# Cross-attention on one core: value stores issued from ScalarE's queue, loads alone on the sync queue, one bias dot moved in each value tile

## What is computed

```python
qp = q @ Wq + bq                      # q = x, [16, 512, 512]
kp = k @ Wk + bk                      # k = v = ctx, [16, 77, 512]
vp = v @ Wv + bv
w = softmax(einsum('bqd,bkd->bqk', qp, kp) / sqrt(512))
x = einsum('bqk,bkd->bqd', w, vp)
gate = concatenate((qp, x), -1) @ Wg + bg
return x * mask * sigmoid(gate) + q
```

## Time and profile before

| | |
|---|---|
| median of 3 runs | 413.2 us (412.16 to 413.94) |
| the profiled execution, device time | 413.69 us |
| its span in the profile | 411.9 us |
| TensorE matmuls busy | 395.4 us, 96% of the span |
| VectorE busy | 273.2 us, 66% |
| ScalarE busy | 229.6 us, 56% |
| GpSimd busy | 133.3 us, 32% |
| DMA, mean over the span | 223 GB/s |
| matmuls on the chain that ended last | 82% of the span |
| DMA on that chain | 5%, of which `sb_row<-sb_dram` 4% |

### The profile page before, as it was taken

One profiled execution on the slowest core, in us unless ns is written; L12 is line 12 of the kernel. 1 busy time (PEld: TensorE's weight loads), 2 busy tenths in 40 slices (PEclk: granted clock), 3 DMA queues, 4 the chain that ended last, 5 costly groups with the idle time before them and its releaser, 6 DMA issues.

```text
span 411.9 us, 7362 instructions
## 1 busy us (share of the span) xinstructions
PE 395.4 (96%) x2386; PEld 361.6 (88%) x2386; DVE 273.2 (66%) x646; ACT 229.6 (56%) x587; POOL 133.3 (32%) x115
## 2 busy tenths in 40 slices
PE   8999999999993999999999999999999999999993
PEld 4889986777783999999999999999999999999992
DVE  3687558774424667667677676676777766767766
ACT  5644242223313666766666667666666676666643
POOL 0004125434823633243242432423334233333100
PEclk9999999999997999999999999999999999999998
DMA  7993533457496779878788786888978879777321
GB/s 269 390 405 142 148 122 121 155 194 265 142 326 249 227 239 278 236 246 231 229 248 229 251 244 219 236 235 243 250 215 248 241 240 232 233 237 237 113 77 76
DMA packets 42660, 91.79 MB, mean 223 GB/s; under 512 B 4633, under 2 KB 4633, under 8 KB 41983
## 3 DMA queue, kind: packets, MB, share of 16 engines
q1 hardware_dynamic: 41471, 89.23, 69.5%
q10 hardware_dynamic: 1152, 2.10, 1.5%
HBM read 64.30 MB, written 27.01 MB: 222 GB/s over the span
## 4 chain that ended last, share of the span: by engine, by line
PE 82%; DVE 5%; DMA 5%; issue 3%; ACT 3%; POOL 1%; SPq 0%; DVEq 0%; ACTq 0%
PE psum L421 50%; PE psum L341 13%; DMA sb_row<-sb_dram 4%; PE psum L448 4%; PE psum L454 4%; PE psum L447 3%; PE psum L453 3%; PE psum L364 3%; DVE dot_tmp L641 3%; PE psum L433 2%; DMA wkT_raw<-in_wkT 1%; ACT vT L490 1%; POOL v_st L818 1%; POOL xT L818 1%; DVE vg_f L726 1%
## 5 line engine op out<-in xcount | busy, mean ns | idle before, releaser
L421 PE MATMUL psum<-ws,xT 128*128 128x296 f32 x1536 | 229.7, 304 | 0.0
L421 PEld LDWEIGHTS psum<-ws,xT 128*128 128x128 f32 x1536 | 220.8, 190 | 5.6
L818 POOL TENSOR_TENSOR xT<-x_raw,xT 128x512 fp32r<-128x512 f32 x64 | 82.4, 1290 | 150.0 <-ACT xT L608 150.0
L765 DVE SCALAR_TENSOR_TENSOR gx<-psum,rinv,gx 128x512 f32<-128x512 f32 x64 | 48.0, 751 | 50.7 <-PE psum L448 50.7
L600 ACT ACTIVATE tanh_sb<-gx 128x512 f32<-128x512 f32 x64 | 40.5, 633 | 52.7 <-DVE gx L765 52.7
L773 DVE SCALAR_TENSOR_TENSOR prod_sb<-tanh_sb,psum 128x512 f32<-128x512 f32 x64 | 44.1, 689 | 25.3 <-ACT tanh_sb L600 25.3
L568 ACT ACTIVATE gx<-psum 128x512 f32<-128x512 f32 x64 | 38.4, 599 | 39.6 <-DVE sc L741 39.6
L787 DVE SCALAR_TENSOR_TENSOR out_sb<-prod_sb,out_factor,x_rows 128x512 f32<-128x512 f32 x64 | 48.2, 753 | 0.3 <-issue 0.3
L608 ACT ACTIVATE xT<-x_raw 128x512 fp32r<-128x512 f32 x60 | 37.1, 620 | 2.0 <-DMA x_raw<-in_xT 2.0
L341 PE MATMUL psum<-wg,vT 128*128 128x512 f32 (+1 forms) x120 | 29.9, 397 | 1.7 <-DVE vT L636 1.6
L341 PE MATMUL psum<-wv,ctxT 128*128 128x512 f32 (+1 forms) x120 | 30.2, 400 | 0.0
(11 more groups left out here) (76 smaller groups left out, 429.6 us busy)
## 6 DMA issues: line engine op xcount, KB each, us to landing
x_rows<-in_x SPq DMA_DIRECT2D x32, 512.0 KB, 9.5
out_y<-out_sb SPq DMA_DIRECT2D x64, 256.0 KB, 4.9
x_raw<-in_xT SPq DMA_DIRECT2D x60, 256.0 KB, 6.7
v_ext<-v_dram SPq DMA_DIRECT2D x32, 308.0 KB
v_dram<-v_st SPq DMA_DIRECT2D x18, 512.0 KB, 3.3
v_ext<-v_dram SPq DMA_DIRECT2D x16, 204.0 KB
ctxT_raw<-in_ctxT SPq DMA_DIRECT2D x4, 624.0 KB, 10.5
ctx_rows<-in_ctx SPq DMA_DIRECT2D x4, 616.0 KB
```

The lines of the kernel that those rows point to most:

```text
L421: last = pe.matmul(ps[:, h, 0:HN], xT[b % 2][:, s, c, q], ws[b % 2][:, m, c, h, :], start=(c == 0 and (s, m) == PRODUCTS[0]), stop=(c == C ...
L765: dve.scalar_tensor_tensor(gx[:, n % 3, :], vgate_ps[n % 2][:, :], rinv[:, n % T:n % T + 1], gx[:, n % 3, :], ALU.mult, ALU.add).then_inc( ...
L818: pool.tensor_tensor(dst, src, f32(hi_), ALU.subtract).then_inc(made, 1)
```

## The change

- The value stores `store_v` and `store_vg` move from SyncE's program to ScalarE's. In pass k, ScalarE now issues `store_vg(k-2)` behind the high part of `vT`, and `store_v(k)` ahead of the high part of the gate sum. Each waits for GpSimd's low part in ScalarE's queue. The last gate store stays on SyncE.
- SyncE's program holds the loads in one row: `load_xT(0)`, the store of `sb_c`, `v_ext` of the first batch, `sb_row`, the four loads of the second batch's `x_raw` (formerly on ScalarE), the first half of `x_rows`, the last gate store, the second half of `x_rows`, `v_ext` of the second batch.
- On VectorE the third bias dot of a pass moves behind the gate sum.

```diff
@@ -264,16 +264,6 @@
                 for c in chunks:
                     sync.dma_start(x_raw[:, c], io["xT"][b, :, c]).then_inc(xT_in[c], 16)
 
-            def store_v(k):
-                i, n = k % 2, KROWS[k]
-                sync.wait_ge(v_lo, k + 1)
-                sync.dma_start(v_dram[k * P:k * P + n, :, 0:D], f32(v_st[i][0:n, :, 0:D])).then_inc(v_stored[i], 16)
-
-            def store_vg(k):
-                i, n = k % 2, KROWS[k]
-                sync.wait_ge(vg_lo, k + 1)
-                sync.dma_start(v_dram[k * P:k * P + n, :, D:2 * D], f32(v_st[i][0:n, :, D:2 * D])).then_inc(vg_stored[i], 16)
-
             def load_vext(b):
                 i, r = b % 2, b * SP
                 sync.dma_start(f32(v_ext[i][0:S, 0, :]), v_dram[r:r + S, HI, :]).then_inc(vext_in[i], 16)
@@ -289,29 +279,25 @@
                     sync.wait_ge(v_stored[i], 16 * ((tiles + 1 - i) // 2))
                     sync.wait_ge(vg_stored[i], 16 * ((tiles + 1 - i) // 2))
 
-            for k in range(KT):
-                store_v(k)
-                if k >= 1:
-                    store_vg(k - 1)
-                if k == 4:
-                    sync.wait_ge(dots_made, DOT["sb", 3] + 1)
-                    load_xT(0, (0, 1))
-                if k == 5:
-                    load_xT(0, (2, 3))
-                if k == 7:
-                    sync.wait_ge(sb_made, 1)
-                    sync.dma_start(sb_dram, sb_c[:, :]).then_inc(sb_out, 16)
-                    wait_stored(2)
-                    load_vext(0)
-                if k == 8:
-
-                    sync.wait_ge(sb_out, 16)
-                    sync.dma_start(sb_row[:, :, :, :].rearrange("p h k b -> p (h k b)"),
-                                   sb_dram.rearrange("(a k) b -> a (k b)", a=1).broadcast_to([P, KEYS])).then_inc(sb_in, 16)
+            sync.wait_ge(dots_made, DOT["sb", 3] + 1)
+            load_xT(0)
+            sync.wait_ge(sb_made, 1)
+            sync.dma_start(sb_dram, sb_c[:, :]).then_inc(sb_out, 16)
+            wait_stored(2)
+            load_vext(0)
+
+            sync.wait_ge(sb_out, 16)
+            sync.dma_start(sb_row[:, :, :, :].rearrange("p h k b -> p (h k b)"),
+                           sb_dram.rearrange("(a k) b -> a (k b)", a=1).broadcast_to([P, KEYS])).then_inc(sb_in, 16)
+            sync.wait_ge(xT_lo, C)
+            load_xT(1, (0, 1))
+            load_xT(1, (2, 3))
             sync.wait_ge(job_done, J["v", KT - 1] + 1)
-            for h in range(T // 2):
-                load_rows(0, h)
-            store_vg(KT - 1)
+            load_rows(0, 0)
+            sync.wait_ge(vg_lo, KT)
+            n = KROWS[KT - 1]
+            sync.dma_start(v_dram[(KT - 1) * P:KEYS, :, D:2 * D], f32(v_st[(KT - 1) % 2][0:n, :, D:2 * D])).then_inc(vg_stored[(KT - 1) % 2], 16)
+            load_rows(0, 1)
             load_vext(1)
             wait_stored(KT)
             for n in range(1, NT + 3):
@@ -539,13 +525,20 @@
             act.wait_ge(job_done, J["mt", MB * C - 1] + 1)
             for c in range(C):
                 hi(wg2[:, HI, c], wg2_raw[:, c], wg2_hi)
+            def store_v(k):
+                i, n = k % 2, KROWS[k]
+                act.wait_ge(v_lo, k + 1)
+                act.dma_start(v_dram[k * P:k * P + n, :, 0:D], f32(v_st[i][0:n, :, 0:D])).then_inc(v_stored[i], 16)
+
+            def store_vg(k):
+                i, n = k % 2, KROWS[k]
+                act.wait_ge(vg_lo, k + 1)
+                act.dma_start(v_dram[k * P:k * P + n, :, D:2 * D], f32(v_st[i][0:n, :, D:2 * D])).then_inc(vg_stored[i], 16)
+
             for k in range(KT + 1):
                 if k >= 2:
                     vT_hi_of(k - 1)
-                if k == KT - 1:
-                    act.wait_ge(xT_lo, C)
-                    for c in range(C):
-                        act.dma_start(x_raw[:, c], io["xT"][1, :, c]).then_inc(xT_in[c], 16)
+                    store_vg(k - 2)
                 if 1 <= k < KT:
                     v_hi_of(k)
                 if k == 7:
@@ -553,6 +546,8 @@
                     for i in range(2):
                         act.wait_ge(wg2_lo[i], C // 2)
                     xT_hi_of(0)
+                if k < KT:
+                    store_v(k)
                 if k >= 1:
                     n = KROWS[k - 1]
                     act.wait_ge(job_drained, J["vg", k - 1] + 1)
@@ -710,7 +705,7 @@
                     ctx_dot(b)
                 if 1 <= k < KT:
                     add_bv(k)
-                for b in dots_of[k][1:]:
+                for b in dots_of[k][1:2]:
                     ctx_dot(b)
                 if k >= 1:
                     n = KROWS[k - 1]
@@ -724,6 +719,8 @@
                         dve.wait_ge(vg_lo, k - 1)
                     dve.wait_ge(job_done, J["vg", k - 1] + 1)
                     dve.tensor_tensor(vg_f[0:n, :], bank[bank_of(J["vg", k - 1])][0:n, :], btot_row[0:n, :], ALU.add).then_inc(job_drained, 1)
+                for b in dots_of[k][2:]:
+                    ctx_dot(b)
                 if k == SB_TILE:
                     dve.wait_ge(dots_made, DOT["sb", SB_ORDER[-1]] + 1)
                     dve.memset(sb_c[:, :], 0.0).then_inc(sb_filled, 1)
```

## The result

| | median, us | runs |
|---|---|---|
| before | 413.57 | 8 (412.0 to 416.81) |
| changed | 416.2 | 8 (414.2 to 417.17) |

The ratio is 1.0066, 95% interval 1.0034 to 1.0098: slower by two thirds of a per cent, and outside the forecast range of 403.0 to 409.5. The profiled execution of the changed kernel took 416.49 us with a span of 414.7; that of before took 413.69 with 411.9.

The account below looks back on a forecast made before the run. TensorE was taken as the bound, busy but for one hole waiting on sb_row. Terms -6.69 - 1.8 + 0.95 - 1.7 + 0.3 + 0.7 + 0.2 = -8.0 took 413.69 to 405.7 us, range 403.0 to 409.5.

Parts of the forecast that it names:

- the hole and its clock: TensorE's idle at about 124 to 131 us, waiting on sb_row, and the slow clock behind it: both go.
- The terms of -6.69 and -1.8 us: Before the first probabilities' transposition: -6.69 us from sb_row issued earlier, -1.8 us from full clock afterwards.
- the dot and the price of the stores' issue: Value stage: tiles 5.96 us apart instead of 6.38 (-1.7 us); store issues 0.51 us each, pass 1 costing +0.95.
- Hidden too: Value stage, middle tiles: the gate store's issue fits ScalarE's idle stretch and costs nothing unless GpSimd is late.
- the last passes: End of value stage: GpSimd's lag delays ScalarE's stores, 0.55 us for pass 9, 0.1 for pass 8.
- The terms +0.3 and +0.7: Value stage: ScalarE's extra issue time in pass 7, +0.3 us; GpSimd's lag from pass 8 to the last product, +0.7.
- a part of the hole stays: Rival: late landing of the last buffers' stores or sb_row keeps some TensorE idle; 407 to 411 us, chance 0.20.
- the batch loop is bound by TensorE's own matmuls, which nothing here touches: Behind the hole, in the batch loop: TensorE's matmuls set the time, so no gain or loss was expected there.
- What is late next: Start of batch loop: VectorE's 3.45 us copy before the first tile's low probabilities makes TensorE wait, +0.2 us.
- The rival on the slower side: Value tiles become bound by ScalarE's store issues; at 1.82 us an issue 416.9 us, chance 0.03.
- the three signs of being wrong: ScalarE waiting for a DMA at its last high part; value tiles over 6.4 us apart; new wait in first four query tiles.
- The rival section: List of alternatives to the forecast; one cited that v_ext loads of 51 and 19 rows use 3 engines and 1.

Follow-up runs that it names:

- e2: Changed kernel with the v_ext loads cut by rows (64 and 13, 48 and 3, 16 and 3): 405.96 us, ratio 0.9832.
- g1: Changed kernel with v_ext cut, second-batch loads ahead of the last gate store's wait, and both value stores behind vT's high part: 403.68 us, ratio 0.9767.
- h1: Changed kernel with only the first batch's v_ext loads cut by rows: 413.26 us, ratio 0.9985.
- f4: Changed kernel with v_ext cut into as many pieces, but by badly dividing rows (63 and 14, 34 and 17, 17 and 2): 415.51 us, ratio 1.0037.
- e1: Changed kernel with second-half x_rows and second-batch v_ext loads ahead of the wait for the last gate store's data: 409.02 us, ratio 0.9905.
- f1: Changed kernel with v_ext cut by rows and second-batch loads ahead of the last gate store's wait: 405.67 us, ratio 0.9803.
- f2: Kernel before with only the v_ext loads cut by rows: 406.9 us, ratio 0.984.
- f3: Kernel before with v_ext cut by rows and the third bias dot behind the gate sum: 406.6 us, ratio 0.9829.
- h2: Changed kernel with only the second batch's v_ext loads cut by rows: 409.26 us, ratio 0.9886.
- g2: Changed kernel with the third bias dot back ahead of the gate sum: 416.7 us, ratio 1.009.

## Why the prediction was wrong

**Right: the hole and its clock.** `sb_row` was out at 100.12, 3 us before the 103.2 of the forecast, and there at 116.4, before the 119.3 that I had allowed, and the first transposition no longer waited. The terms of -6.69 and -1.8 us came in. With the two losses cured (e2) the profile has the first transposition at 125.09, forecast 124.8, and the time 405.96 (profiled 406.24), forecast 405.7. That agreement is another kernel's: it supports the sizes of these terms, not the forecast of this change.

**Right: the dot and the price of the stores' issue.** Tiles of passes 3 to 6 are 5.96 us apart. An issue on ScalarE took 0.52 us. Pass 1 waits for GpSimd, and its gate high part begins at 67.79, forecast 67.5; TensorE's product there waited 1.31 us where it had 0.32. GpSimd's lateness in the last passes is what is left in e2 as a wait of 1.29, where before had 0.61; g1 removed both.

**Wrong, the first time: "Hidden too" and the last passes.** The step costed the stores' issue and never their landing in the value stage. I had the median of 4.1 us and the 15.2 of the crowd, used the long one only for the very last buffer, and wrote that `v_ext` and `sb_row` would be gone from the queues by then. They were gone by then because they had moved into passes 7 to 9, where each rounding waits for a store of two tiles ago. The terms +0.3 and +0.7 stood for about 4 us: 1.07 and 2.00 of waiting and 1.6 of slow clock in the last product, less the 0.61 that was waited there before. By h1, 3.4 us of it up to the first transposition come from the uncut loads. The rival "a part of the hole stays" had the right mechanism, the wrong buffers, and an end of 412.7 that it does not pass by itself.

**Wrong, the second time: "the batch loop is bound by TensorE's own matmuls, which nothing here touches".** This is the step that decided the sign. The timeline of the kernel before has, beyond the rows that I chose:

```profile
135.76 1.74 SPq L265 DMA_DIRECT2D x_raw<-in_xT  x2
```

```profile
146.37 0.63 ACT L608 ACTIVATE xT<-x_raw 128x512 fp32r<-128x512 f32 x1 [2.00 <-DMA x_raw<-in_xT]
```

ScalarE waited 2.0 us for the very same chunk, without harm to TensorE, and the load stood behind the same five `v_ext` loads, the first of them issued at 130.75. My rows ended at 138 us. The chunk landed at 146.3 before and at 146.8 after, while TensorE came to it 4.2 us earlier, so ScalarE's wait grew from 2.0 to 6.7 and TensorE stood for 4.5. Two tiles cost 7.1 us more than before, against the 4.2 won. "What is late next" was asked of the first tile only; the next late thing stood at the fourth tile. No case that I wrote contained it. The rival on the slower side, ScalarE bound by its issues, named 416.9, and the measured 416.2 is near that by luck alone: an issue took 0.52 us, where that rival needed about 1.7. Of the three signs of being wrong, two were there: tiles over 6.4 us apart (7.20 and 6.98), and a new wait within the first four query tiles. The third was not: at its last high part ScalarE waited 6.1 us, but for VectorE's gate sum and no DMA.

**The rule that was at hand.** The rival section cited the engines that a transfer may use, and set it aside since no row shows single engines. The runs show what was needed: e2 against f4, and the packet counts. By the Trainium skill's rule (DMA: Bandwidth & Descriptors, Why a DMA increments its semaphore by 16 and not by 1), an estimate: the uncut loads of a first use put 52 rows on the lowest engine (7 and 7, 17, 2, 19), those of e2 18, those of f4 70, of a mean of 16 each, and the landing of `sb_row` behind them was 16.3, 6.8 and 18.4 us. The landings of the stores do not keep that order: in f4 they were shorter than in the changed kernel. So that the shape decides is shown, and that it acts through the load of the lowest engines is argued.

## What to carry to other kernels

When a change closes the largest hole, ask of every load that is needed afterwards when it lands now and how much slack it has, through the whole first round of the loop: a transfer that lands at a fixed time turns each microsecond won ahead of it into waiting, and its slack is read in the trace of before as a harmless wait on a side engine. A store that frees a buffer counts as such a load. Before transfers are reordered, look at their row counts: cutting 77, 51 and 19 rows into multiples of 16 and small rests was worth 1.6% in the kernel before and 2.3% in the changed one. Without the cut, the change with its new order cost 0.7%, and e1's order gained 1.0% on the kernel before. With the cut, e2, f1, f2 and f3 lie between 0.980 and 0.984 of before whatever their order, and g1, whose later stores also spare ScalarE a wait, at 0.977.

## What the runs showed of the hardware that I had not expected

- The same bytes in nine DMAs gave 405.96 us cut as 64 + 13, 48 + 3 and 16 + 3 rows, and 415.51 us cut as 63 + 14, 34 + 17 and 17 + 2.
- The 868, 388 and 70 added small packets come out if each `v_ext` load has one packet of under 512 B for each DMA engine that it uses. Read so, the packet count tells whether a cut has spread a load.
- The window's mean DMA share told little of it: from 104 to 112 us the changed kernel had a share of 0.88 and 311 GB/s, e2 0.99 and 330, 6% apart, while stores issued in it took up to 11.5 us to land.
- The clock does not answer alike to the same wait. The last gate product stood behind 2.0 us of idle in four kernels: it took 4.55 us in the changed kernel and 4.25 in h2, and 2.98 in e1 and 2.97 in g2. So part of the first loss, some 1.5 us, need not be there in each execution. The changed kernel's eight runs fit that: the two with a mean granted clock of 0.987 took 414.2 and 414.85 us, the one with 0.986 took 416.05, and the five with 0.982 or 0.983 took 416.16 to 417.17.
